# Two audio encoder layers in one program: the gating, ordering and return of the chosen-token layer

## What is computed

```python
k = 748 * 2 // 8                                  # 187 tokens for each expert
S = softmax(x @ Wg)                               # x = layernorm(h); 8 experts
G, I = top_k(S.T, k)                              # for each sequence and expert
ex = x[I]                                         # the chosen rows
hmid = gelu(ex @ W1[e] + b1[e])                   # 128 -> 256, exact gelu
out = hmid @ W2[e] + b2[e]                        # 256 -> 128
new_x = zeros_like(x).at[I].add(G[..., None] * out)
h = h + new_x
```

## Time and profile before

| | us |
|---|---|
| median of 3 runs | 2848.66 (2844.8 to 2848.93) |
| the profiled execution, its own time | 2844.66 |
| its span | 2842.9 |
| `choose`: the list rounds (lines 1270, 1272) | 1233.8 to 1280.9 of the span |
| `chosen_ffn` | 1286 to 1746 of the span |

### The profile page before, as it was taken

The page is one execution under the profiler, slowest core; times in us unless marked ns, Lnnn a source line. Parts: engine busy times, 40 slices in busy tenths (PEclk is TensorE's granted clock), DMA queues, the critical chain, the costliest instruction groups (busy, mean ns, idle before and its releaser), DMA issues. The chain is left out here.

```text
span 2842.9 us, 53155 instructions
## 1 busy us (share of the span) xinstructions
PE 2453.6 (86%) x16811; PEld 1874.4 (66%) x16811; DVE 2100.0 (74%) x3869; ACT 1761.4 (62%) x3324; POOL 1060.1 (37%) x1210
## 2 busy tenths in 40 slices
PE   7979699999999997547888886888749997999993
PEld 7969454444444443436888885888637885888882
DVE  4545589999999994895888785677676664777775
ACT  3336177777777777425777773444437885777772
POOL 0025012222323233334444441333326775566664
PEclk9989699999999998758999997999979998999997
DMA  3109523333333330541111112300002111677748
GB/s 82 38 9 357 141 46 55 55 58 58 58 58 58 58 58 12 148 139 33 34 31 33 32 31 96 110 0 0 1 0 104 49 48 56 217 245 246 240 154 259
DMA packets 161301, 249.24 MB, mean 88 GB/s; under 512 B 41644, under 2 KB 106901, under 8 KB 154232
## 3 DMA queue, kind: packets, MB, share of 16 engines
q1 hardware_dynamic: 128888, 208.77, 27.2%
q0 software_dynamic: 19712, 38.13, 4.3%
q10 hardware_dynamic: 12544, 0.39, 0.2%
HBM read 155.24 MB, written 93.41 MB: 87 GB/s over the span
## 5 line engine op out<-in xcount | busy, mean ns | idle before, releaser
L1054 ACT ACTIVATE probs<-score 128x748 f32<-128x748 f32 (+1 forms) x768 | 568.3, 794 | 117.0 <-PE score L879 115.7
L983 DVE TENSOR_REDUCE part_max<-to_dve 128x1 f32<-128x512 f32 (+1 forms) x768 | 480.1, 684 | 83.4 <-PE to_dve L860 83.0
L2735 DVE TENSOR_TENSOR m_hid_lo<-m_hid,m_hid_hi 128x512 fp32r<-128x512 f32 x408 | 288.0, 707 | 158.5 <-ACT m_hid_hi L2708 158.5
L860 PE MATMUL to_dve<-k_stack,q_stack 48*128 48x512 f32 (+3 forms) x1536 | 351.5, 367 | 21.6 <-DMA k_stack<-k_parts 20.7
L879 PE MATMUL score<-q_stack,k_stack 49*128 49x374 f32 (+1 forms) x1536 | 317.4, 389 | 3.1 <-ACT probs L1054 1.0
L916 PE MATMUL o_sum<-probs,v_sb 128*17 128x374 f32 (+1 forms) x3072 | 315.6, 483 | 0.1
L879 PEld LDWEIGHTS score<-q_stack,k_stack 49*128 49x128 f32 (+1 forms) x1536 | 162.0, 181 | 225.0 <-ACT probs L1054 199.7
L1383 POOL DMA_INDIRECT f_row_in_c<-c_rows,c_ids x192 | 187.6, 977 | 258.9 <-DVE f_gated_c L1529 191.7
L860 PEld LDWEIGHTS to_dve<-k_stack,q_stack 48*128 48x128 f32 (+1 forms) x1536 | 223.0, 187 | 80.7 <-DVE part_max L983 36.7
L2631 POOL DMA_INDIRECT e_sums<-m_gated,m_row_in x216 | 212.5, 984 | 162.7 <-DVE m_gated L2753 101.8
L2708 ACT CAST m_hid_hi<-m_hid 128x512 fp32r<-128x512 f32 x408 | 248.3, 609 | 0.0
(11 more groups left out here) (449 smaller groups left out, 6158.3 us busy)
## 6 DMA issues: line engine op xcount, KB each, us to landing
m_weights<-e_records SPq DMA_DIRECT2D x54, 1028.0 KB, 6.6
q_stack<-q_parts SPq DMA_DIRECT2D x192, 93.5 KB, 3.1
k_stack<-k_parts SPq DMA_DIRECT2D x192, 93.5 KB, 4.2
e_slots<-blank SPq DMA_DIRECT2D x54, 260.0 KB, 3.7
m_row_in<-e_slots SPq DMA_DIRECT2D x54, 260.0 KB, 2.9
m_weights<-e_sums SPq DMA_DIRECT2D x16, 640.0 KB
e_records<-l_parts SPq DMA_DIRECT2D x16, 512.0 KB, 4.1
v_rows<-v_out SPq DMA_DIRECT2D x16, 408.0 KB, 6.0
```

The costliest lines, as they stand in the source:

```text
L860: last = pe.matmul(ring[i % RING][0:ROWS[c], at_col:at_col + keys.stop - keys.start], q_stack[its_slot][rows, j, c * P:c * P + ROWS[c]], k ...
L983: dve.tensor_reduce(part_max[0:ROWS[c], k, j, c, 0:1], ring[i % RING][0:ROWS[c], :], AX.X, ALU.max).then_inc(used, 1)
L1054: act.activation(probs[0:n, s % 2, m, 2 * j:2 * j + 2, :], score[tile][0:n, :, 0:HALF], ACT.Exp).then_inc(tile_used, 1)
L2735: dve.tensor_tensor(hid_lo[:, f % RING, :], hid[:, f % RING, :], hid_hi[:, f % RING, :].bitcast(F32), ALU.subtract).then_inc(lo_done, 1)
```

## The change

Five edits.

1. **List rounds.** Round r of the second 24 reads and writes columns 8r to 8r + 569 (at most to 748) in place of all 748.
2. **Gates.** GpSimd, three units behind its gathers, picks each row's gate: it multiplies the two candidate gates of each of the three tiles by a 0/1 matrix `owner` (128 x 6 numbers) and adds the pairs (128 x 3). The gathers of unit n now wait for `turned` of unit n - 5 in place of `gated_n`.
3. **Gated rows in whole-unit operations.** VectorE multiplies the turned-back rows by the gates in one operation of 128 x 384 (`weigh`), ScalarE rounds in one (`round_gated`), VectorE subtracts in one (`split_gated`). Before: four and four. VectorE's queue becomes `weigh`, `give_back` or mark 0, `split_gated`, (mark 0), mark 1, split_hid 0, mark 2, split_x, split_hid 1, `measure`.
4. **TensorE's order.** `turn_rows(k+1)` stands before all of `combine(k-2)`, which is in one piece.
5. **The return** is in four operations in place of eight, over tiles 0 to 4 and tile 5 for each half, and `combine` of a new sequence waits for all of it.

```diff
                 for r in range(SLOTS_E // 8):
                     some = key[:, 8 * r:8 * r + 8]
-                    then(dve.max(some, work[:, :]))
+                    window = work[:, 8 * r:min(T, 8 * r + 8 + T - k_tokens)]
+                    then(dve.max(some, window))
                     if r < SLOTS_E // 8 - 1:
-                        then(dve.match_replace(work[:, :], some, work[:, :], -1.0))
+                        then(dve.match_replace(window, some, window, -1.0))
...
+                def gather(n):
                     if n >= RING:
-                        pool.wait_ge(gated_n, n - RING + 1)
+                        pool.wait_ge(turned, n - RING + 1)
...
+                def pick_gate(n):
+                    pool.wait_ge(gathered[n % RING], 16 * UNIT_TILES * (n // RING + 1))
+                    first = P + experts_of(n)[0]
+                    if n:
+                        pool.wait_ge(gate_made, n)
+                    pool.tensor_tensor(either[:, :, :], row_in[:, n % RING, :, first:first + 2], owner[:, :, :], ALU.mult
+                                       ).then_inc(picked, 1)
+                    if n >= 2:
+                        pool.wait_ge(weighed_n, n - 1)
+                    pool.wait_ge(picked, n + 1)
+                    pool.tensor_tensor(gate[:, n % 2, :], either[:, :, 0], either[:, :, 1], ALU.add).then_inc(gate_made, 1)
+
+                pool.wait_ge(owned, 2 * UNIT_TILES + 2)
+                for k in range(UNITS_C + PICK_BEHIND):
+                    if valid(k - PICK_BEHIND):
+                        pick_gate(k - PICK_BEHIND)
+                    if valid(k):
+                        gather(k)
...
                 def turn_back(n):
                     pe.wait_ge(kept, 2 * n + 2)
                     if n:
-                        pe.wait_ge(gated_n, n)
+                        pe.wait_ge(weighed_n, n)
...
+                    if i == 0 and b:
+                        pe.wait_ge(added, b)
                     for c in tiles:
-                        if i == 0 and b and c % 2 == 0:
-                            pe.wait_ge(added, BANKS * (b - 1) + c // 2 + 1)
...
-                    if valid(k - 2):
-                        combine(k - 2, range(0, TILES // 2))
                     if valid(k + 1):
                         turn_rows(k + 1)
                     if valid(k - 2):
-                        combine(k - 2, range(TILES // 2, TILES))
+                        combine(k - 2, range(TILES))
...
-                    for part in gate_parts(n):
-                        at, tile, e = part
-                        act.activation(gated[at, n % 2, tile, 0, :], back[at, tile, :], ACT.Identity, bias=zero[at, :],
-                                       scale=gate_of(n, part)).then_inc(gate_hi, 1)
+                    act.copy(gated[:, n % 2, :, 0, :], weighed[:, n % 2, :, :]).then_inc(gate_hi, 1)
...
-                def gate_rows(n):
-                    dve.wait_ge(gate_hi, GATES * (n + 1))
-                    for part in gate_parts(n):
...
+                def weigh(n):
+                    dve.wait_ge(turned_back, n + 1)
+                    dve.wait_ge(gate_made, n + 1)
+                    if n >= 2:
+                        dve.wait_ge(gated_n, n - 1)
+                    dve.tensor_tensor(weighed[:, n % 2, :, :], back[:, :, :],
+                                      gate[:, n % 2, :].unsqueeze(2).broadcast_to([P, UNIT_TILES, P]), ALU.mult
+                                      ).then_inc(weighed_n, 1)
+
+                def split_gated(n):
+                    dve.wait_ge(gate_hi, n + 1)
+                    dve.tensor_tensor(gated[:, n % 2, :, 1, :], weighed[:, n % 2, :, :],
+                                      gated[:, n % 2, :, 0, :].bitcast(F32), ALU.subtract).then_inc(gated_n, 1)
...
-                        for c0, c1, n in PARTS_B:
+                        for c0, c1, n in [(0, TILES - 1, P), (TILES - 1, TILES, LAST)]:
...
-                dve.memset(zero[:, :], 0.0).then_inc(zeroed, 1)
+                for j, rows_at, mine in [(0, slice(0, P), 0), (1, slice(0, H), 0), (1, slice(H, P), 1), (2, slice(0, P), 1)]:
+                    dve.memset(owner[rows_at, j, mine:mine + 1], 1.0).then_inc(owned, 1)
+                    dve.memset(owner[rows_at, j, 1 - mine:2 - mine], 0.0).then_inc(owned, 1)
```

More of the change, by code:

```diff
@@ L1345, in chosen_ffn @@
         marks = sb("f_marks", [P, 2, UNIT_TILES, T], F32R)
-        zero = sb("f_zero", [P, 1])
+        weighed = sb("f_weighed", [P, 2, UNIT_TILES, P])
+        either = sb("f_either", [P, UNIT_TILES, 2])
+        owner = sb("f_owner", [P, UNIT_TILES, 2])
+        gate = sb("f_gate", [P, 2, UNIT_TILES])
         turn = ps("f_turn", [P, 512])
@@ L1349, in chosen_ffn @@
         down, back = ps("f_down", [P, 512]), ps("f_back", [P, UNIT_TILES, P])
-        sums = [ps(f"f_sums{k}", [P, 2, 2, P]) for k in range(BANKS)]
-        (turned, rounded, split, up_done, gelu_done, hi_done, lo_done, down_done, kept, turned_back, gate_hi, gated_n,
-         marked, combined, half_added, added, zeroed) = (
+        sums = ps("f_sums", [P, BANKS, 2, 2, P])
+        (turned, rounded, split, up_done, gelu_done, hi_done, lo_done, down_done, kept, turned_back, weighed_n, gate_hi, gated_n,
+         marked, combined, half_added, added, owned, picked, gate_made) = (
             sem(s) for s in ("f_turned", "f_rounded", "f_split", "f_up_done", "f_gelu_done", "f_hi_done", "f_lo_done",
-                             "f_down_done", "f_kept", "f_turned_back", "f_gate_hi", "f_gated", "f_marked", "f_combined",
-                             "f_half_added", "f_added", "f_zeroed"))
+                             "f_down_done", "f_kept", "f_turned_back", "f_weighed_n", "f_gate_hi", "f_gated", "f_marked", "f_combined",
+                             "f_half_added", "f_added", "f_owned", "f_picked", "f_gate_made"))
         gathered = [sem(f"f_gathered{k}") for k in range(RING)]
-        GATES = 4
         def experts_of(n):
             return [2 * (n % PER_BATCH) + e for e in range(2)]
[L1363 to L1368, removed]
-            at, tile, e = part
-            return row_in[at, n % RING, tile, P + e:P + e + 1]
+        PICK_BEHIND = 3
         def valid(n):
@@ L1546, in give_back @@
                             dve.wait_ge(half_added, b + 1)
[L1547 removed]
+                        for c0, c1, n in [(0, TILES - 1, P), (TILES - 1, TILES, LAST)]:
                             h = g.h[0:n, b * TILES + c0:b * TILES + c1, :]
[L1549 to L1553 removed]
+                            last = dve.tensor_tensor(h, h, flat[0:n, c0:c1, half, :], ALU.add)
+                        last.then_inc(added if half else half_added, 1)
                 def measure(b):
[L1556 removed]
+                    dve.wait_ge(added, b + 1)
                     take_statistics(dve, g, b, range(TILES))
[L1559 removed]
+                for j, rows_at, mine in [(0, slice(0, P), 0), (1, slice(0, H), 0), (1, slice(H, P), 1), (2, slice(0, P), 1)]:
+                    dve.memset(owner[rows_at, j, mine:mine + 1], 1.0).then_inc(owned, 1)
+                    dve.memset(owner[rows_at, j, 1 - mine:2 - mine], 0.0).then_inc(owned, 1)
                 for k in range(-1, UNITS_C + 2):
@@ L1562, in _ @@
                     if valid(k - 2):
-                        gate_rows(k - 2)
+                        weigh(k - 2)
                     if done is not None:
                         give_back(done // PER_BATCH)
-                    if valid(k - 1):
+                    elif valid(k - 1):
                         mark(k - 1, 0)
-                    if valid(k):
-                        split_hid(k, 0)
+                    if valid(k - 2):
+                        split_gated(k - 2)
+                    if done is not None and valid(k - 1):
+                        mark(k - 1, 0)
                     if valid(k - 1):
@@ L1572, in _ @@
                     if valid(k):
-                        split_hid(k, 1)
+                        split_hid(k, 0)
                     if valid(k - 1):
@@ L1577, in _ @@
                         split_x(k + 1)
+                    if valid(k):
+                        split_hid(k, 1)
                     if done is not None:
```

24 lines of the change are left out of this document (5 added, 19 removed).

## The result

| | before | after |
|---|---|---|
| median of 4 runs, us | 2846.73 | 2769.59 (2768.31 to 2772.89) |
| the profiled execution, us | 2844.66 | 2772.89 |
| its span, us | 2842.9 | 2771.2 |

The ratio is 0.9731, 95% interval 0.9714 to 0.9748: faster, 77 us by the medians and 71.7 by the two spans. The forecast said 2785. The rest is which executions were profiled: the one of the changed kernel is the slowest of its four, 3.3 above their median.

The account below looks back on a forecast made before the run. A loop of gates, sums and turn back was taken as the bound; 8.4 (rounds) + 51.2 (units) + 3.2 (ends) - 0.5 (memsets) = 62.3 us off 2844.66, adjusted to the median, gave 2785 us, range 2772 to 2797 (with A and B 2770 to 2810).

Parts of the forecast that it names:

- What bounds the kernel: Chosen-token layer: no engine full; a loop of gates, sums and turn back sets the 6.29 us unit, links adding to 6.2.
- List rounds: Second 24 list rounds: priced by the column, fewer columns save 8.4 us, ends 0 and 10.5.
- Ordinary unit: Units without return or statistics: TensorE's own queue becomes the bound, 6.29 falls to 5.45 us, 0.84 saved a unit.
- cover of x: Ordinary unit: x is ready for widen 0.26 us before TensorE is free.
- The two units at a sequence's end: Return unit falls from 7.87 to 6.3 us, the unit behind the statistics from 6.61 to 6.55.
- The ends: Layer's last two units, with nothing beside them, and the last return: a shorter chain saves 3.2 us.
- GpSimd, at no cost: GpSimd's two picks, about 0.5 us a unit with the wait, fit its idle time: 4.3 is under 5.45.
- The wait itself: At the return, waiting for all three banks of added costs nothing, since split_gated comes later still.
- A: Rival, chosen-token units: VectorE and ScalarE, not TensorE, set the unit; ordinary units 5.85 us, total 2807 us; chance 0.17.
- B: Rival, list rounds: they don't get cheaper with fewer columns, 8.4 us back, total 2793 us; chance 0.06.
- C: Rival, GpSimd: picks ahead of the gathers make it the bound, a unit 7.3 us, slower at 2870 us; chance 0.04.
- D: Rival, chosen-token loop: widen waits on something else, unit stays 6.29 us, total about 2838 us; chance 0.03.

Follow-up runs that it names:

- E2: Kernel before with only GpSimd-picked gates, whole-unit gated-row operations and VectorE's new order; old TensorE order, return and rounds: ratio to before 0.9814.
- E1: Kernel before with only the second 24 list rounds narrowed to 569 columns: ratio to before 0.9964; rounds 38.42 us in place of 47.15.
- E6: Changed kernel plus a ScalarE copy of 128 x 384 (0.41 us) ahead of the rounding of x: ratio to before 0.9769, 11 us slower than the changed kernel.
- E7: Changed kernel without four of the twelve products of narrow in each unit, 0.45 us less on TensorE: ratio to before 0.9691, 11 us faster than the changed kernel.
- E4: Changed kernel with TensorE's old order, the turn between two halves of the sums: ratio to before 0.9764, 9 us slower than the changed kernel.
- E5: Changed kernel with the old return, eight operations with a wait for each bank: ratio to before 0.973; a sequence of 23.32 us.
- E8: Changed kernel gathering only the first five units, the others reading the same rows again: ratio to before 0.9723; a sequence of 23.07 us.
- E10: Changed kernel with a sequence's six statistics spread over the next two iterations, plus 28 transposes at the layer's start: ratio to before 0.9704.
- the repeat of the changed kernel: The changed kernel unaltered, timed again on another chip against the kernel before: ratio 0.9738, a sequence of 23.40 us.

## Why the forecast held, and where it was short

1. **What bounds the kernel.** Right: the loop gates, sums, turn back. E2 takes it away and wins 45.5 us, and no ordinary unit of 6.29 is left. How much of that is VectorE's new order no run shows.
2. **List rounds.** 8.4 forecast, 8.7 measured; E1 has the same rounds by themselves.
3. **Ordinary unit.** 5.45 forecast, 5.47 measured, cover of x 0.26 forecast, 0.39 by the walk of the trace and 0.29 by E6. That TensorE is the bound is shown from both sides, by E6 and E7.
4. **The two units at a sequence's end: the term that was mis-sized.** 6.3 and 6.55 forecast, 5.91 and 6.31 measured, 0.63 a sequence or 9.8 us over 15.5 sequences; the 62 units as a whole fell 9.2 short. In the first the walk was right up to the end of `split_gated` (3.3 forecast, 3.31 measured from the start of `widen`). Behind it I put three marks, split_hid 0 and `split_x` at 2.9, which is the sum of their lengths even with short marks (3 x 0.6 + 0.57 + 0.54), and then 0.1 for long marks. They took 2.55 (3.31 to 5.86). The step that failed is the sum of lengths: I took off the overlap of 0.07 between neighbours for the four returns and forgot it for these five operations, 0.35; the 0.1 for long marks was not needed either, and against both stand 0.05 of handing over. In the second, `weigh` started 1.51 behind `widen` (1401.19 - 1399.68) in place of 1.65, and the chain from it to the next `widen` took 4.80, not 4.91. The clock adds to this and takes from it. Two falls of it lengthened the kernel before by some 1.9 us in these units, one of them the sequence of 28.22, and this was saved through the clock and not through the loop. The first gap between turn backs, at a low clock, was 9.21 us where 5.45 is the steady one, and 7.13 where 6.29 is: 2.9 us lost again.
5. **The ends.** 3.2 forecast, 5.4 measured. The rest is TensorE's clock, which the forecast left out. The last but one sums of the layer took 3.81 us before, the last 4.21 (first line); then the last two of the changed kernel:

```profile
1737.79 4.21 PE L1437 MATMUL f_sums_c<-f_gated_c,f_marks_c 128*128 128x256 f32 x18 [3.23 <-DVE f_gated_c L1529]
...
1661.75 2.41 PE L1452 MATMUL f_sums_c<-f_gated_c,f_marks_c 128*128 128x256 f32 x18 [0.17 <-DVE f_gated_c L1545]
...
1666.27 3.34 PE L1452 MATMUL f_sums_c<-f_gated_c,f_marks_c 128*128 128x256 f32 x18 [1.79 <-DVE f_gated_c L1545]
```

Together 8.02 before and 5.75 after, 2.3 less, which is about the difference. The chain is shorter, and the first of them came before the clock fell (last section). I had not forecast this part of the gain.
6. **GpSimd, at no cost.** Right; the pick took 0.24 and 0.41 us on average in place of 0.2 each, and `weigh` never waited for it: the gate was made over 9 us before.
7. **The turn and the return.** I costed them within the whole and not alone. E4 gives the turn 9 to 12 us, E5 the return and the wait for all banks together 3 us by the trace and nothing that the timing can tell. The wait itself was free, as forecast: the return ended at 1419.78, and the first sums, at 1420.30, waited for the gated rows, ready at 1420.24:

```profile
1420.30 2.18 PEld L1452 LDWEIGHTS f_sums_c<-f_gated_c,f_marks_c 128*128 128x128 f32 x18 [0.34 <-DVE f_gated_c L1545]
```

8. **Small terms.** The sum gives 2844.66 - 62.3 + 4.0 = 2786.4, which I rounded down to 2785. Most of the errors lay on one side; the 2.9 us of the layer's start alone made up for a part of them.

Against the rivals: A is out by the unit at 5.47 and by E6, B by the rounds at 753 and 737 ns, C by the unit at 5.47, D by E2.

## What to carry to other kernels

When no engine is full, write down the loop whose links add up to the beat: here ScalarE, VectorE, TensorE and back, 6.2 of 6.29 us. Shortening it pays until the next thing, so work out that one too, with its cover, and ask which unit of a pattern is bound by which engine: a product less on TensorE paid in two units of four, and six small operations dealt out to the next two iterations paid 0.8 us a sequence. An edit's worth depends on what else is bound: the same turn was worth 3 us on one kernel and 12 on the other. And when you add up a full queue, take off what neighbours overlap, 0.07 us each here.

## What the runs showed of the hardware

**GpSimd and VectorE's marks hold each other up.** GpSimd's timeline of the changed kernel, the second pick operation and the gathers behind it, and one mark of VectorE:

```profile
1412.40 0.49 POOL L1393 TENSOR_TENSOR f_gate_c<-f_either_c 128x3 f32<-128x3 f32 x1 [0.81 <-DVE f_weighed_c L1539]
1413.04 1.25 POOL L1379 DMA_INDIRECT f_row_in_c<-c_rows,c_ids  x1 [0.15 <-issue]
1414.60 0.94 POOL L1379 DMA_INDIRECT f_row_in_c<-c_rows,c_ids  x1 [0.30 <-issue]
...
1415.11 0.80 DVE L1552 TENSOR_SCALAR f_marks_c<-c_ramp,c_keys_at 128x748 fp32r<-128x748 f32 x1
...
1417.88 0.19 POOL L1393 TENSOR_TENSOR f_gate_c<-f_either_c 128x3 f32<-128x3 f32 x1 [0.82 <-DVE f_weighed_c L1539]
```

The 128 x 3 sum at 1412.40 takes 0.49 and ends at 1412.89, 0.05 behind a mark of VectorE that ran from 1412.24 to 1412.84; the one at 1417.88, beside the return, takes 0.19. Of the 64 sums 47 began during a mark, and each took 0.48 to 0.49 and ended 0.05 behind it. With the gathers, who loses goes in this trace with where in the gather the mark begins: 45 marks began 0.3 to 0.4 us into a gather, took their 0.60, and the gather took 1.25 in place of 0.94; 43 marks began 0.5 us into one, as the one at 1415.11 did, took 0.80, and the gather kept its 0.94. The long ones are nearly all the third mark of a unit; at the return the marks stayed at 0.59 to 0.64. Once the gathers are gone all are at 0.60 (E8). The Trainium skill, SBUF — State Buffer, "SBUF: two separate sides", states that VectorE (in a two-port mode or with two SBUF inputs) and GpSimd hold their shared ports as an exclusive lock for a whole instruction. For the small sum the trace agrees, with 0.3 us lost up to the mark's end; in the other direction it does not, for the marks never lost as much as a gather lasts, 0.94, but 0.2.

**TensorE's clock at the two ends of the layer.** Windows of before (first) and of the changed kernel; PEclk is the last but two:

```profile
1301.00:1306.00 5.00, 4.41 (x27) 3.93 (x26) 1.34 (x3) 3.30 (x10) 3.94 (x4) 0.75 0.22 59
1716.00:1720.00 4.00, 3.24 (x15) 3.27 (x16) 3.80 (x10) 0.72 (x3) 0.00 (x0) 0.57 0.00 0
1728.00:1732.00 4.00, 2.09 (x12) 1.92 (x12) 2.86 (x7) 1.57 (x5) 0.00 (x0) 0.77 0.00 0
```

```profile
1299.00:1304.00 5.00, 4.53 (x21) 4.14 (x20) 3.14 (x7) 2.60 (x7) 3.35 (x5) 0.50 0.15 37
1304.00:1309.00 5.00, 5.00 (x39) 5.00 (x38) 2.70 (x6) 1.58 (x5) 1.29 (x3) 0.84 0.11 28
...
1660.00:1664.00 4.00, 3.81 (x31) 3.67 (x31) 2.67 (x5) 1.25 (x3) 0.00 (x0) 1.00 0.00 0
```

Before, the clock fell twice inside the layer, both times at a return's wait (0.50 in 1636 to 1638, 0.57 in 1716 to 1720), and to 0.77 and below in the last two units, whose chain left TensorE idle for 1.9 us and more. The sequence around the first fall took 28.22 us, the others near 27.06. After, it stayed at 1.00 from the fourth unit to the sums of the last but one. At the start it went the other way: TensorE began its work 11 us before the clock was full in the kernel before, and some 20 in the changed one, at one window of 0.50 and the next of 0.84. The gap between the first two turn backs was 7.13 and 9.21 us, and from 6.50 to 10.28 in the other kernels' executions. I have no cause for this spread; E10 shows only that early work alone doesn't end it. Nor is the clock all of it: in the repeat of the changed kernel and in E10, ScalarE stood idle for 3.22 and 3.15 us in this stretch, ahead of the first `keep`, and the trace shows nothing that it waited for. It is some 3 us of noise in every comparison of traces here.
